# Masking two of eight local score units on GpSimd after the exponential, instead of on TensorE before it

## The reference

```python
mask = jnp.triu(jnp.ones((window, window), dtype=q.dtype), k=1)
scores = jnp.einsum('bhqd,bhkd->bhqk', q, k) * scale + mask
a = jax.nn.softmax(scores, axis=-1)
o = jnp.einsum('bhqk,bhkd->bhqd', a, v).transpose(0, 2, 1, 3).reshape(B, T, D)
...
lqs = x @ proj_local
gqs = x @ proj_global
local_out = _sliding_window_attn(lqs, Wl_in, bl_in, Wl_out, bl_out, LOCAL_W)
global_out = _sliding_window_attn(gqs, Wg_in, bg_in, Wg_out, bg_out, GLOBAL_W)
fused = w[0] * local_out + w[1] * global_out
```

## Time and profile before

| | |
|---|---|
| time, median of 3 runs | 1631.32 us (1628.41 to 1633.1) |
| time of the profiled execution | 1638.02 us |
| its span, first to last instruction | 1636.3 us |
| mean granted TensorE clock | 0.969 |
| PE / DVE / ACT / POOL busy | 92% / 76% / 56% / 44% |
| identity matmuls of local units (L1245) | 256, eight in each of 32 steps |

### The profile page before, as it was taken

One profiled execution on the slowest core, in us unless ns is written; L12 is line 12 of the kernel. 1 busy time (PEld: TensorE's weight loads), 2 busy tenths in 40 slices (PEclk: granted clock), 3 DMA queues, 4 the chain that ended last, 5 costly groups with the idle time before them and its releaser, 6 DMA issues.

```text
span 1636.3 us, 39878 instructions
## 1 busy us (share of the span) xinstructions
PE 1510.0 (92%) x13672; PEld 1095.4 (67%) x13672; DVE 1238.9 (76%) x3785; ACT 913.6 (56%) x1919; POOL 723.6 (44%) x1097
## 2 busy tenths in 40 slices
PE   5799999999999999999999999999999854999993
PEld 3567777777777777777777777777776633777772
DVE  2577888888888888788888888888888642788883
ACT  3256666666666666666666666666666532222220
POOL 2113444444444444444444444444444341466666
PEclk9899999999999999999999999999999976999997
DMA  6887666665666665556665555665555203355540
GB/s 126 159 223 191 109 111 100 109 107 105 108 106 107 107 105 105 101 102 105 106 104 101 102 100 101 107 103 103 101 97 98 79 23 102 121 154 170 180 137 11
DMA packets 253720, 183.56 MB, mean 112 GB/s; under 512 B 29492, under 2 KB 252151, under 8 KB 253518
## 3 DMA queue, kind: packets, MB, share of 16 engines
q1 hardware_dynamic: 232414, 164.49, 52.1%
q10 hardware_dynamic: 14192, 12.79, 2.9%
q0 software_dynamic: 6912, 3.73, 0.8%
HBM read 55.78 MB, written 38.04 MB: 57 GB/s over the span
## 4 chain that ended last, share of the span: by engine, by line
PE 55%; SPq 12%; POOL 10%; issue 7%; DVE 6%; DMA 6%; ACT 1%; ACTq 1%; POOLq 0%; DVEq 0%
SPq L400 12%; PE bank L1288 9%; PE bank L1439 9%; PE bank L1398 8%; DMA stack<-mT 5%; PE bank L1319 5%; PE bank L1257 4%; PE bank L1278 3%; PE bank L1270 3%; PE bank L1254 2%; PE bank L1295 2%; POOL rstd L517 2%; POOL xrow L587 2%; POOL slots_scratch L576 2%; PE bank L1452 2%
## 5 line engine op out<-in xcount | busy, mean ns | idle before, releaser
L922 DVE TENSOR_REDUCE mx<-bank 128x2 f32<-128x512 f32 (+1 forms) x768 | 513.9, 673 | 187.3 <-PE bank L1316 99.2
L688 ACT ACTIVATE pt<-bank 128x512 f32<-128x512 f32 x768 | 449.8, 593 | 262.2 <-PE bank L1257 177.0
L1288 PE MATMUL bank<-xnT,weff 128*128 128x256 f32 x1024 | 256.7, 395 | 7.2 <-DVE rest L906 6.4
L1288 PEld LDWEIGHTS bank<-xnT,weff 128*128 128x128 f32 x1024 | 188.5, 194 | 42.9 <-issue 11.9
L1319 PE MATMUL bank<-stack 96*128 96x256 bf16 x1024 | 197.5, 274 | 5.4 <-DVE mx L922 5.1
L1257 PE MATMUL bank<-stack 100*128 100x128 bf16 x2048 | 198.4, 218 | 0.0
L539 POOL TENSOR_TENSOR parts<-rest,parts 128x512 bf16<-128x512 f32 x128 | 147.1, 1158 | 84.2 <-ACT parts L705 84.2
L554 POOL TENSOR_TENSOR obuf<-obuf,xrow 128x512 f32<-128x512 f32 x32 | 40.6, 1269 | 296.6 <-ACT obuf L730 296.6
L1257 PEld LDWEIGHTS bank<-stack 100*128 100x128 bf16 x2048 | 158.1, 97 | 12.7
L699 ACT ACTIVATE parts<-bank,bqk 128x256 bf16<-128x256 f32 x256 | 107.2, 469 | 103.5 <-PE bank L1288 103.4
L1254 PE MATMUL bank<-tri,identb 128*128 128x256 bf16 x512 | 140.8, 275 | 23.0 <-DMA stack<-mT 21.1
(11 more groups left out here) (153 smaller groups left out, 2720.9 us busy)
## 6 DMA issues: line engine op xcount, KB each, us to landing
stack<-parts SPq DMA_DIRECT2D x768, 64.0 KB, 2.6
stack<-parts SPq DMA_DIRECT2D x378, 128.0 KB, 5.4
slots_scratch<-zeros ACTq DMA_DIRECT2D x16, 650.0 KB, 5.6
xr<-x SPq DMA_DIRECT2D x32, 256.0 KB, 7.9
out<-obuf SPq DMA_DIRECT2D x32, 256.0 KB, 2.2
ew<-w_gate SPq DMA_DIRECT2D x32, 256.0 KB, 3.9
ew<-w_up SPq DMA_DIRECT2D x32, 256.0 KB, 5.2
ew<-w_down SPq DMA_DIRECT2D x32, 256.0 KB, 4.3
```

Of the source, the lines that this page charges most:

```text
L688: act.activation(pt[:, u % 8, :], S2[u % 2][:, :], ACT.Exp).then_inc(p_ready, 1)
L922: dve.reduce_max(dst, src, AX.X).then_inc(s1_read, 1)
L1288: last = pe.matmul(bank[:, t * WIN:(t + 1) * WIN], weff[:, b, c, qk * D + t * P:qk * D + (t + 1) * P], xnT[:, par, c, :], start=(c == 0), ...
```

## The change

In stage c the local units 6 and 7 lose their identity matmul; their four score matmuls now each open and close their own 128 columns. POOL multiplies the exponentials of these two units by e where the mask is one (`etri` holds e above the diagonal and 1 elsewhere; exp(s + 1) = e exp(s)). `values(3)`, which reads units 6 and 7, waits for POOL (`p_masked`) instead of ACT. POOL's two multiplications a step stand behind `low_part(1)`, ahead of `inv_std(1)`. Two operations at the start make `etri`.

```diff
+    PU = 6
...
+        etri = sb("etri", [P, P])
...
+            pool.memset(etri[:, :], math.e)
...
+            pool.affine_select(out=etri[:, :], in_=etri[:, :], compare_op=ALU.is_gt, fill=1.0,
+                               base=0, pattern=[[-1, P]], channel_multiplier=1)
...
+            def masked(u, c):
+
+                wait(pool, p_ready, c, UNITS, u)
+                pool.tensor_tensor(pt[:, u, :].rearrange("p (a n) -> p a n", n=P), pt[:, u, :].rearrange("p (a n) -> p a n", n=P),
+                                   etri[:, :].unsqueeze(1).to_broadcast([P, 4, P]), ALU.mult).then_inc(p_masked, 1)
...
                 if a:
                     low_part(0, a)
                     low_part(1, a)
+                if c:
+                    for u in range(PU, LU):
+                        masked(u, c)
                 if d:
                     inv_std(1, d)
...
                 if u < LU:
-                    pe.matmul(bank[:, :], identb[:, :], tri[:, :].unsqueeze(1).to_broadcast([P, 4, P]), start=True, stop=False)
+                    if u < PU:
+                        pe.matmul(bank[:, :], identb[:, :], tri[:, :].unsqueeze(1).to_broadcast([P, 4, P]), start=True, stop=False)
...
                             last = pe.matmul(bank[:, (2 * h2 + j) * P:(2 * h2 + j + 1) * P], k_stack(par, 0, h, j * P, P),
-                                             q_stack(par, 0, h, j * P, P), start=False, stop=(h2 == 1 and j == 1))
+                                             q_stack(par, 0, h, j * P, P), start=(u >= PU),
+                                             stop=(u >= PU or h2 == 1 and j == 1))
...
                 if g < 4:
-                    wait(pe, p_ready, c, UNITS, 2 * g + 1)
+                    if 2 * g + 1 < PU:
+                        wait(pe, p_ready, c, UNITS, 2 * g + 1)
+                    else:
+                        wait(pe, p_masked, c, LU - PU, 2 * g + 1 - PU)
```

More of the change, by code:

```diff
@@ L1 @@
+import math
 import concourse.bass as bass
@@ L223, in attention_moe_program @@
         p_ready = sem("p_ready")
+        p_masked = sem("p_masked")
         pv_full = sem("pv_full")
```

## The result

The changed kernel takes 1639.88 us, median of 11 runs (1636.81 to 1647.34); the kernel before, run beside it, 1630.91 (1628.41 to 1637.99). The ratio is 1.0058, 95% interval 1.0040 to 1.0075: slower by 9 us, where 1640 was predicted. The profiled execution took 1639.51 us, close to that median.

The account below looks back on a forecast made before the run. The prediction took the loop from unit 8 through the last `low_part`, SP's queue and the maxima's landing as the bound; -0.3 + 1.5 + 8 = +9 us on the median 1631.3 gave 1640 us, range 1628 to 1651.

Parts of the forecast that it names:

- The loop: Unit 8 to last `low_part` 27.1 us, SP's issues 8.5 to 10.1, landing 2.7 to 3.0, then unit 8 again.
- total wait of 33 us or more: PE's wait for the maxima at unit 8 was to total this in place of 21.1 us.
- 38.6 plus the wait: Length of steps in which PE waits at unit 8; steps without a wait last 38.6 us.
- The saving that becomes wait (-0.3 us): PE's 0.44 us a step saved ahead of unit 8 turn into longer wait there; -0.3 us is kept.
- The products on POOL: POOL's two multiplications take 2.5 us, fit its idle time and end before `values(3)`, so the new wait costs nothing.
- DVE held by POOL (+1.5 us): After unit 8, POOL's products hold up a DVE TENSOR_SCALAR in about eight steps, 0.1 to 0.35 us each.
- The clock (+8 us): Longer waits at unit 8 let PE fall to half clock more often, 1.66 us each; bounds 0 and +23.
- sixteen waits of 1.1 us and more: Count of such waits before unit 8, instead of five, with two in five followed by half clock.
- No change: Rival: the saving becomes wait at unit 8 and the clock falls no more often; 1631 to 1635 us, chance 0.32.
- Faster: Rival: the wait at unit 8 shrinks along with PE's work; 1617 us wholly true, 1624 half true, chance 0.08.
- The port: Rival: POOL's products hold up DVE after unit 8 in every step, 0.3 to 0.9 us each; about 1650, chance 0.12.

Follow-up runs that it names:

- Experiment 4: The DMA of the global row maxima issued earlier in SP's queue: in the kernel before 1620.72 us (0.9913), in the changed kernel 1625.54 us (0.9938).
- PE's part alone: Kernel before without the identity products of units 6 and 7, POOL multiplying nothing (mask missing): 1641.54 us, ratio 1.0055.
- experiment 1: Kernel before without identity products and without POOL's multiplications (mask missing): two units 1641.54 us (1.0055), four units 1661.05 us (1.0178).
- experiment 6: Changed kernel with unit 6's product ahead of the `obuf` sum: 1640.19 us; also with maxima issued earlier: 1592.55; early issue without POOL's products: 1593.82.
- POOL's part alone: Kernel before with all identity products kept, POOL also multiplying units 6 and 7 by ones: 1632.88 us, ratio 1.0013.
- experiment 7: Kernel before with the DMA of the global row maxima issued earlier, run a second time in its own set: 1620.89 us, ratio 0.9915.
- `before_sp`: Kernel before with the DMA of the global row maxima issued earlier in SP's queue: 1620.72 us (0.9913), in a second set 1620.89 us (0.9915).
- experiment 5: Kernel before with two useless matmuls ahead of the wait at unit 8: 1639.82 us (1.0035); the changed kernel again, same chip: 1640.11 us (1.0030).
- the best kernel: Changed kernel with unit 6's product ahead of the `obuf` sum and the global row maxima issued earlier: 1592.55 us, ratio 0.9772.

## Why the prediction held

**The loop.** Right. The first part from unit 8 to the last `low_part` stayed at 27.1 us, and the issues and the landing go on as before. I expected a total wait of 33 us or more; it is 30.1. The missing 3 us are SP's: issues and landing together took 0.16 us a step less in this execution than in that of before (9.21 and 2.85 us against 9.33 and 2.88), and so the landing came nearer to PE. My "38.6 plus the wait" was 0.17 us short for every step with a wait: the step that I showed lasts 39.69 us with 0.92 of wait. The wait is counted from the recorded end of the last matmul, 0.39 us behind its start, where the next one could have started 0.22 behind it. It changes nothing in the sum. Experiment 4 shows that the loop goes over SP's queue: one block of issues moved behind the maxima takes 14 us from the kernel before and all but removes the wait.

**The saving that becomes wait (-0.3 us).** Right: PE's part alone gives no gain (experiment 1), and the steps are 0.43 us shorter than PE's 38.6 as soon as nothing else sets them (experiment 6).

**The products on POOL.** I took 2.5 us for two; the rows of the changed kernel, products (ns, min/median/max) and `L945`, say 1.27 each. The new wait of `values(3)` for POOL is not among PE's waits.

```profile
L547 POOL TENSOR_TENSOR pt<-pt,etri x64: 1257/1266/1276, 90.3 to 1308.4; 128x512 f32<-128x512 f32 x64
...
L945 DVE TENSOR_SCALAR mparts<-mx x64: 147/170/1107, 54.5 to 1297.1; 128x32 bf16<-128x32 f32 x64
```

**DVE held by POOL (+1.5 us).** Right in mechanism; the size is not resolved. Between 300 and 1300 us `L945` took 421 to 639 ns in five steps, and the first parts of four of them were 27.2 to 27.3 us long: 0.7 us in all. In the steps at full clock the products end 7.44 us after unit 8 less the step's wait, 7.0 and 6.7 us where I had said 6.9 and 6.6, and `L945` starts 6.59 us after unit 8. Of these 7.44 us, 0.2 are an operation that grew longer, which I did not see coming (last section). `L989`, from which I argued, takes 206 to 1144 ns under a low part, always until that low part ends, and not 1144 whenever one is running. In the trace of POOL's part alone seventeen are held, up to 856 ns, as its products come later against unit 8 without PE's saving; that kernel's 2 us, with an interval from 0 to 4.7, are an upper value and can't be told from nothing. The full form of this rival, priced at 0.3 to 0.9 us a step, came about in experiment 4, where the wait was gone and the products ran into the operation in every step: 4.8 us more than the kernel before with the same early issue on the same chip, although PE has 14 us less to do. The Trainium skill (SBUF — State Buffer, "Who interferes with whom") has the later of the two blocked for the whole instruction of the earlier; the 1.07 us of `L946`, which ends with the product, agree.

**The clock (+8 us).** Right, and the term that decides. It came from two events in one trace; six comparisons now carry it. Twice the removed work gives a mean clock that accounts for 31.3 of 31.2 us; two units give 9.6 of 11.7; filling the gap with useless matmuls gives all back at a mean clock of 0.9713; POOL's part alone leaves the clock as it was; and the changed kernel on a second chip and with one product moved on a third lose 5.3 and 10.8 us where their clocks give 5.0 and 11.3. Part of the count was off: I forecast sixteen waits of 1.1 us and more with two in five followed by a slow stretch. The profile has nine such waits, in part for SP's shorter issues, and four of them went with a slow stretch; the timed runs lost 6.7 stretches against the kernel before by their mean clock, where I took 4.4 and rounded the cost up. That nothing happens below 1.1 us, as the sixteen waits took for granted, was wrong: the fifth stretch of this profile came after a wait of 0.92 us, and one of experiment 1 after 0.86 us. Nor is a long wait enough by itself: 1.10 us at 206.62 was followed by a stretch, 1.61 us at 600.42 was not. With four units, and waits of 1.3 us on average, nineteen stretches stand against five long waits without one. What decides between two such waits no run here shows. PE's timeline of the changed kernel at the shortest:

```profile
1305.42 0.28 PE L1272 MATMUL bank<-tri,identb 128*128 128x256 bf16 x1 [0.92 <-DMA stack<-mT]
...
1305.77 3.58 PE L1419 MATMUL bank<-wo,OnT 128*128 128x256 f32 x8
```

The Trainium skill (TensorE: Matmul & The Clock Gate, "HAM oscillation — how this bites in real kernels") blames waits for DMAs between short runs of matmuls, longer ones than these, and counts half of the throttled time as lost. That half agrees: the step after 718.58 lost 28.77 - 27.09 = 1.68 us by a stretch of about 3.4 us. That a single wait of about a microsecond in 39 us of dense work can be enough is what the runs add.

**The sum.** PE's part alone +9 us and POOL's +2 us, by their ratios, against +9.4, +4.9 and (with the product moved) +11.2 us in three measurements of the whole. The parts add up within their intervals. My three terms, -0.3, +1.5 and +8, gave the median of the changed kernel to a microsecond, which is luck beyond what the terms deserve: the clock's +8 came from sixteen long waits where the profile has nine, and the measured differences go from 5 to 11 us.

**The rivals.** *No change* fell: its condition, that the clock falls no more often, did not hold. *Faster* fell with experiment 1. *The port* was real, and small in the changed kernel as it stands.

**What stays open.** The late start of DVE behind the seventh group of values (experiment 7) was found in five traces from two chips and in none of nine from the others. It costs about 0.4 us a step where PE is otherwise the bound, and so would explain the 39.0 us of `before_sp`, and part of the loss in experiment 5. It may also be why the changed kernel waits and loses less on its chip (22.5 us of wait and 5 us, against 30.1 and 9); that is not tested. For the changed kernel the instructions are the same with and without it, so something outside them matters. For the kernel before with the early issue only the late kind was seen; whether it reaches 38.6 us on a chip without it was not shown, and neither was whether the 1592.55 us of the best kernel hold on a chip that has it. Ends of matmuls are modelled, so it may be PE that is late there, or its signal.

## What to carry to other kernels

Ask of each wait of the busiest engine which loop it closes: PE was busy 92%, yet its work ahead of the wait was worth nothing until one DMA issue stood a few places earlier in its queue. Shortening an engine's work ahead of such a wait is not neutral on TensorE, since a longer gap can cost granted clock (here 1.66 us each time, after waits of 0.86 us and more), and the price falls behind the wait, on the path. When an operation moves to GpSimd, choose its place by what DVE does at that moment, not only by where GpSimd is idle: the same two products cost nothing in one place and hold up a 0.17-us operation for a microsecond in another.

## What was not expected of the hardware

POOL's `obuf` sum grew from 1268 to 1475 ns in nearly every step. It now starts while DVE runs `On` (L979): at 718.28 us, with `On` from 718.22 to 718.63. In the kernel before `On` (L963) starts 0.28 us ahead of it instead of 0.06, and it takes 1268 ns. The nine traces of kernels that lack the identity products of units 6 and 7 at their places all show 1475 ns in 29 of the 32 steps, and the five of kernels that have them none. That DVE holds POOL there is read from this overlap, not tested. It is not free: the low parts and the products follow it without a gap and so end 0.2 us later. Where the products ended 6.97 us after unit 8 the first part was 27.1 us, and where they ended 7.09 to 7.19 us after it 27.2 to 27.3. So I estimate that without these 0.2 us the four steps that lost time by `L945` would have lost next to none.

```profile
L567 POOL TENSOR_TENSOR obuf<-obuf,xrow x32: 1263/1475/1482, 167.1 to 1361.7; 128x512 f32<-128x512 f32 x32
```

Two matmuls whose result nobody reads took the whole loss of 9 us back in the changed kernel (1.0005 against 1.0058), and cost 5 us in the kernel before, on another chip. And the changed kernel has DVE start 0.07 us behind a group of matmuls in one set and about 0.87 us behind it on the chip of another, in nearly every step.
